# Phi less its first feature is made during the cross attention and kept in DRAM; a row of ones is set by a VectorE eviction

## The chip, the cores and the metric

The kernel runs on one core of one Trainium2 chip, as one program. The metric is the device time of the core in microseconds. Before the change three timed runs gave 577.39, 581.51 and 581.21 us (median 581.21). PE is TensorE, DVE is VectorE, ACT is ScalarE, POOL is GpSimd, and SP is the queue that issues every DMA here.

## The reference, cut to what matters

Three residual steps on x (4 batches x 256 tokens x 256 features), each on the layer norm of x:

```
x = x + xattn(ln(x), ctx)    # one head over 4096 context rows a batch, in f32
x = x + attn(ln(x))          # causal, 16 heads of 16
x = x + ffn(ln(x))           # soft mixture of 64 experts x 32 slots

# ffn:
logits = ln(x) @ phi_w.T + phi_b          # phi_w 2048 x 256, phi_b 2048
D = softmax(logits over the 32 slots);  C = softmax(logits over the 64 experts)
X = D' x -> clip -> norm -> tanh -> expert_w, expert_b -> C mixes the experts' outputs
```

The features of a normed token sum to zero. So every column of phi_w may have its first feature subtracted from all features without changing the logits, and the first feature's row, now zero, is free to carry phi_b, if the first feature of every token is replaced by a one. "Phi less its first feature" is that product: `phi - phi[0]` with row 0 of its first half replaced by phi_b.

## The kernel before, in words

There are three stages, each a block of five engine programs written out in order, and no engine starts a stage before all have ended the one before.

**Cross attention** (`cross_attention`) walks over 4 batches x 8 context chunks of 512 rows. Each chunk comes by two DMAs on SP: turned (512 KB, L325, used for the scores) and plain (512 KB, L321, used for the mix). Both have a ring of four slots. ACT rounds each to f32r (L661, L666), POOL makes the low part (L380, L385), PE multiplies. The low part of turned chunk n+2 and the plain chunk n-6 are made in POOL's iteration n. SP's iteration n loads plain chunk n-6, which waits until the low part four chunks back is done, and turned chunk n. At n = 16, 18 and 20 SP also issues the loads of the self-attention's weights.

**Self attention** (`self_attention`) goes through 16 groups G of 4 heads (4 groups a batch). For each group PE makes the scores, DVE the maxima (L1391), ACT the exponentials with their sums (L1327, L1333), DVE the reciprocals (L1399), POOL multiplies (`normalise(G)`: L1077 then L1080), PE turns the result (L1203, L1204, L1208; here T(G)), ACT and DVE move it to SBUF (L1340, L1404), PE mixes the values. In iteration i the engines do: PE scores of i+2, T(i), mix(i-1); POOL normalise(i+1), at some i the padding of values (L1071), and for i >= 8 `less_first_column(i-8)` (L1090), a subtraction on 128x512 of phi; DVE the maxima of i+2, the evictions of T(i), the maxima of i+3, and in i = 8 and 12 `normed(0)` and `normed(1)` (L1444), the normed tokens of a batch; in i = 6, 10, 14 `add_output`. ACT does the exponentials of i+2 before its eviction of T(i). Phi itself (2 MB, L1053) and its first row broadcast (1 MB, L1054) are loaded on SP when the scores of group 7 are made, `less_first_column` waits for both, and when four of the eight are done phi_b is loaded over row 0 (L1056). At the end POOL writes ones into row 0 of the first half of the turned tokens (L1128).

**Soft mixture** (`soft_moe`) goes through 32 logit units u (token tile x 512 columns): PE (L1740), ACT eviction (L1858), DVE maximum, subtraction, sum and reciprocal (L1945, L1950, L1957, L1962), ACT exponential, POOL division (L1666), PE partial products (L1747). Tokens of the second half are turned by PE after unit 4 (L1732); DVE evicts the first feature half (L1988) as step v = 5, POOL then writes a row of ones into it (L1701), and PE waits for that before it goes on after unit 7.

Of the kernel before, what the change touches and what calls it, by code (L numbers as in the profile page):

```python
# [41 lines left out]
           "phi_in", "x_one_g") + tuple(f"rows_in{k}" for k in range(8))  # L42
# [166 lines left out]
def cross_attention(nc, x_sb, x_stats, x_mv, ident, kept, x_rows, ctx, ctx_turned, w_qk_rows, b_rows, Wv, Wo, bo,  # L209
                    c_attn_w, c_attn_b, c_proj_w, c_proj_b, qk_dram):  # L210

    SCALE = 1.0 / 16.0
    ATT_SCALE = 16 ** -0.5
    RING = 3
    with ExitStack() as st:
# [25 lines left out]
        mv = early[:, DH * D + D + 6 * TT:DH * D + D + 8 * TT].rearrange("p (t e) -> p t e", e=2)  # L241
        ve = sb("ve", [P, TT])
# [32 lines left out]
        wq_a = sem("wq_a")  # L275
# [40 lines left out]
        def _(sp):  # L316
# [10 lines left out]

            def weight(w, a, done):
                sp.dma_start(w_nat[w], a.rearrange("(j p) d -> p j d", p=P)).then_inc(done, 16)
# [29 lines left out]
            for s in range(3):  # L359
                store_parts(sp, kept, qk_dram, parts(s), s)  # L360
                if s == 0:
                    sp.wait_ge(ctxTlo_g, NCH * B)
                if s < 2:
                    stack_rows(sp, kept, qk_dram, q_rows, k_rows, s)

        @block.gpsimd
        def _(pool):
# [32 lines left out]
            for n in range(NCH, B * NCH):  # L400
# [572 lines left out]
def self_attention(nc, x_sb, x_stats, x_mv, x_ve, x_rstd, ident, kept, more, qk_dram, phi_turned, phi_b):  # L973
# [4 lines left out]
    with ExitStack() as st:  # L978
# [57 lines left out]
        SL = phi_b.shape[0]  # L1036
        phi_row = more[:, 4, :]
        phi_in, phi_g, x_one_g = kept.sem["phi_in"], sem("phi_g"), kept.sem["x_one_g"]
# [4 lines left out]
        def _(sp):  # L1043
# [9 lines left out]
            sp.dma_start(kept.front[:], phi_turned).then_inc(phi_in, 16)  # L1053
            sp.dma_start(phi_row, phi_turned[0:1, 0:SL].broadcast_to([P, SL])).then_inc(phi_in, 16)  # L1054
            sp.wait_ge(phi_g, SL // 512)
            sp.dma_start(kept.front[0:1, 0:SL], phi_b.rearrange("(o s) -> o s", o=1)).then_inc(phi_in, 16)  # L1056
            sp.wait_ge(phi_in, 48)

        @block.gpsimd
        def _(pool):  # L1060
# [43 lines left out]
            for i in range(GROUPS):  # L1104
# [20 lines left out]
                if i >= GROUPS // 2:  # L1125
                    less_first_column(i - GROUPS // 2)
# [382 lines left out]
def soft_moe(nc, x_sb, x_stats, x_mv, x_ve, x_rstd, ident, kept, disp, expert_w, expert_b, out):  # L1509
# [18 lines left out]
    with ExitStack() as st:  # L1528
# [10 lines left out]
        power = sb("power3", [P, QT])  # L1539
        sstats = sb("sstats", [P, 2, 6])  # L1540
# [115 lines left out]
        def _(pool):  # L1656
# [71 lines left out]
        def _(pe):  # L1728
# [64 lines left out]
            for u in range(NU):  # L1793
                if u == 3:
                    pe.wait_ge(kept.sem["out_v"], B)
                logit(u)
# [3 lines left out]
                if u == LB + 3:  # L1800
                    pe.wait_ge(x_one_g, 2)
# [128 lines left out]
        def _(dve):  # L1930
# [4 lines left out]

            add_projection(dve, nc, kept, x_sb, B - 1)
# [41 lines left out]
            for v in range(NU + 1):  # L1978
# [57 lines left out]
def perceiver_block(nc, x_rows, ctx, ctx_turned, w_qk_rows, b_rows, Wv, Wo, bo, c_attn_w, c_attn_b, c_proj_w, c_proj_b,  # L2036
                    phi_turned, phi_b, expert_w, expert_b, out):
    SL = phi_b.shape[0]
    with ExitStack() as st:
# [13 lines left out]
        qk_dram = nc.dram_tensor("qk_parts_dram", (2 * DH, 2, NPART, P, HALF), BF16).ap()  # L2053
        with ExitStack() as until_moe:
            kept = carried_tensors(nc, until_moe, bank, front, back, first, phib, wide, turned)
            cross_attention(nc, x_sb, x_stats, x_mv, ident, kept, x_rows, ctx, ctx_turned, w_qk_rows, b_rows, Wv, Wo, bo,
                            c_attn_w, c_attn_b, c_proj_w, c_proj_b, qk_dram)
            more = st.enter_context(nc.sbuf_tensor("more", [P, TT - 2, SL], F32))
            self_attention(nc, x_sb, x_stats, x_mv, x_ve, x_rstd, ident, kept, more, qk_dram, phi_turned, phi_b)
# [28 lines left out]
```

## Time and profile before

| | us |
|---|---|
| timed runs | 577.39, 581.51, 581.21 (median 581.21) |
| profiled execution, its own time | 578.23 |
| its span | 576.4 |
| PE busy | 541.2 (94%) |
| DVE / ACT / POOL busy | 345.5 / 357.7 / 350.6 |
| mean granted TensorE clock | 0.994 of full |

The span is from the first to the last instruction of one execution taken by the hardware profiler; the 1.8 us beside it are start and end. Busy shares are averages over the three stages, which lie at 0 to 262 us, 262 to 362 us and 362 to 576 us. PE is busy nearly throughout the first and the third; in the second its slices go down to 7 or 8 tenths.

### The profile page before, as it was taken

To read this page: it belongs to the slowest core of one execution; us is meant where nothing else is said; L and a number is where in the kernel's file an instruction comes from. 1 tells how busy PE (TensorE), PEld (TensorE's weight loads), DVE (VectorE), ACT (ScalarE), POOL (GpSimd) and SP (SyncE) were. 2 spreads that over 40 slices of the span, in tenths; PEclk is the share of its full clock that TensorE was granted. 3 is DMA by queue.
4 is the path that set the end of the run, shared out by engine and by line. 5 is a ranking of instruction groups with operands and counts; after the bars stand their busy time and mean duration, and the time that the engine had idled before them with its cause. 6 is when DMAs were issued, how large, how long until landed. Compare 5 with 4: busy or idle time off the path is not lost. (4 is left out here: it accounts for less than half of the span.)

```text
span 576.4 us, 9531 instructions
## 1 busy us (share of the span) xinstructions
PE 541.2 (94%) x3384; PEld 429.5 (75%) x3384; DVE 345.5 (60%) x695; ACT 357.7 (62%) x1000; POOL 350.6 (61%) x271
## 2 busy tenths in 40 slices
PE   5998999999999999998997977879999999999998
PEld 4786998999899999887666655445555886777786
DVE  1784444464456445536787896787999999334100
ACT  2437665766576857853887973339999885554300
POOL 2775986667666764644579697244576889906000
PEclk9999999999999999999899998999999999999999
DMA  8454445454434333176069400400000907877100
GB/s 290 155 220 147 147 146 182 149 202 146 162 131 146 146 117 103 48 148 136 2 169 213 168 2 0 148 1 1 0 1 1 195 24 232 280 218 221 38 19 18
DMA packets 37056, 70.22 MB, mean 122 GB/s; under 512 B 3217, under 2 KB 27153, under 8 KB 35985
## 3 DMA queue, kind: packets, MB, share of 16 engines
q1 hardware_dynamic: 37010, 69.62, 39.3%
q8 instruction: 27, 0.44, 0.3%
q14 instruction: 19, 0.16, 0.1%
HBM read 65.42 MB, written 4.19 MB: 121 GB/s over the span
## 5 line engine op out<-in xcount | busy, mean ns | idle before, releaser
L380 POOL TENSOR_TENSOR ctxT_lo<-front,ctxT_hi 128x1024 fp32r<-128x1024 f32 x32 | 76.8, 2405 | 55.3 <-ACT ctxT_hi L661 55.3
L385 POOL TENSOR_TENSOR ctx_lo<-ctx_in,ctx_hi 128x1024 fp32r<-128x1024 f32 x32 | 76.7, 2400 | 17.2 <-ACT ctx_hi L666 17.2
L494 PE MATMUL ps<-ctx_hi,pT_hi 128*128 128x256 f32 x256 | 75.4, 295 | 1.8 <-DVE pT_lo L832 1.8
L496 PE MATMUL ps<-ctx_hi,pT_lo 128*128 128x256 f32 x256 | 72.4, 283 | 0.0
L495 PE MATMUL ps<-ctx_lo,pT_hi 128*128 128x256 f32 x256 | 72.3, 283 | 0.0
L685 ACT CAST pT_hi<-ps 128x512 fp32r<-128x512 f32 x64 | 34.0, 591 | 42.1 <-PE ps L476 42.1
L1740 PE MATMUL ps<-front,turned 128*128 128x512 f32 x128 | 59.7, 593 | 0.3 <-PEq L978 0.3
L1788 PE MATMUL ps<-front,comb 128*128 128x256 f32 x256 | 57.8, 381 | 0.0
L824 DVE TENSOR_SCALAR_CACHE_REDUCE first<-ps,qbk 128x512 f32<-128x512 f32 x32 | 24.0, 750 | 55.5 <-PE ps L464 53.1
L1788 PEld LDWEIGHTS ps<-front,comb 128*128 128x128 f32 x256 | 47.6, 190 | 7.6 <-issue 1.6
L832 DVE TENSOR_TENSOR pT_lo<-ps,pT_hi 128x512 fp32r<-128x512 f32 x64 | 41.1, 686 | 17.4 <-ACT pT_hi L685 17.4
L494 PEld LDWEIGHTS ps<-ctx_hi,pT_hi 128*128 128x128 f32 x256 | 49.0, 191 | 2.8 <-DVE pT_lo L832 2.5
L1869 ACT ACTIVATE comb<-comb,cneg 128x64 f32<-128x64 f32 x128 | 51.0, 417 | 0.0
L1679 POOL TENSOR_TENSOR comb<-comb,cinv 128x512 f32<-128x512 f32 x32 | 40.2, 1283 | 15.5 <-DVE cinv L1975 15.5
L495 PEld LDWEIGHTS ps<-ctx_lo,pT_hi 128*128 128x128 f32 x256 | 49.1, 192 | 0.1
L496 PEld LDWEIGHTS ps<-ctx_hi,pT_lo 128*128 128x128 f32 x256 | 49.0, 191 | 0.0
L464 PE MATMUL ps<-ctxT_hi,qk_hi 128*128 128x512 f32 x128 | 40.7, 400 | 2.6 <-DVE qk_lo L816 2.2
L464 PE MATMUL ps<-ctxT_lo,qk_hi 128*128 128x512 f32 x128 | 39.7, 391 | 0.0
L464 PE MATMUL ps<-ctxT_hi,qk_lo 128*128 128x512 f32 x128 | 39.7, 391 | 0.0
L1740 PEld LDWEIGHTS ps<-front,turned 128*128 128x128 f32 x128 | 24.1, 190 | 19.4 <-issue 17.9
L1666 POOL TENSOR_TENSOR more<-more,dinv 128x512 f32<-128x512 f32 x24 | 25.1, 1048 | 19.6 <-DVE dinv L1962 19.6
L661 ACT CAST ctxT_hi<-front 128x1024 fp32r<-128x1024 f32 x32 | 33.8, 1060 | 5.1 <-PE ps L464 3.8
(235 smaller groups left out, 1345.2 us busy)
## 6 DMA issues: line engine op xcount, KB each, us to landing
front<-in_ctx_turned_dram SPq DMA_DIRECT2D x32, 512.0 KB, 4.3
ctx_in<-in_ctx_dram SPq DMA_DIRECT2D x32, 512.0 KB, 3.3
back<-in_L_ffn_expert_w_dram SPq DMA_DIRECT2D x11, 1024.0 KB, 5.5
turned<-in_L_ffn_expert_w_dram SPq DMA_DIRECT2D x5, 1024.0 KB, 7.7
front<-in_phi_turned_dram SPq DMA_DIRECT2D x1, 2048.0 KB
front<-in_L_ffn_expert_b_dram SPq DMA_DIRECT2D x4, 512.0 KB, 10.3
qk_parts_dram<-first SPq DMA_DIRECT2D x4, 384.0 KB, 5.1
qk_parts_dram<-qk_parts SPq DMA_DIRECT2D x4, 384.0 KB, 2.9
```

Source lines behind the costliest of these rows:

```text
L380: nc.gpsimd.tensor_tensor(ctxT_lo[:, n % RING, :, :], turned_in[:, n % SLOTS, :, :], ctxT_hi[:, n % RING, :, :].bitcast(F32), ALU.subtract ...
L385: nc.gpsimd.tensor_tensor(ctx_lo[:, m % RING, :], ctx_in_sb[:, m % SLOTS, :], ctx_hi[:, m % RING, :].bitcast(F32), ALU.subtract).then_inc( ...
L464: last = nc.tensor.matmul(pS[q][:], a[:, dh, q * P:(q + 1) * P], k[:, n % RING, dh, :], start=step == 0, stop=step == 5)
L494: nc.tensor.matmul(pO[q][:, 0:D], pT_hi[:, c % 2, q, cols], hi, start=c == 0 and j == 0, stop=False)
L495: nc.tensor.matmul(pO[q][:, 0:D], pT_hi[:, c % 2, q, cols], lo, start=False, stop=False)
L496: last = nc.tensor.matmul(pO[q][:, 0:D], pT_lo[:, c % 2, q, cols], hi, start=False, stop=c == NCH - 1 and j == J - 1)
L685: nc.scalar.copy(pT_hi[:, c % 2, q, :], probs_banks(c)[q][:]).then_inc(probsThi_a, 1)
L832: nc.vector.tensor_tensor(pT_lo[:, c % 2, q, :], probs_banks(c)[q][:], pT_hi[:, c % 2, q, :].bitcast(F32), ALU.subtract).then_inc(probsTlo ...
L1679: nc.gpsimd.tensor_tensor(part, part, cinv[:, c, :].unsqueeze(1).broadcast_to([P, EB, NS]), ALU.mult).then_inc(cmul_g, 1)
L1740: last = nc.tensor.matmul(psL[u % 4][:], hT[:, c, t * P:(t + 1) * P], phiT[:, c, cols], start=c == 0, stop=c == DH - 1)
L1788: last = nc.tensor.matmul(psY[t], comb[:, t, s * P:(s + 1) * P], mixed[:, s, :], start=s == 0 and (t >= TT // 2 or t % 2 == 0), stop=s == ...
L1869: nc.scalar.activation(column, column, ACT.Exp, bias=cneg[:, c, p:p + 1], accum_out=csum[:, c, p:p + 1]).then_inc(cslot_a, 1)
```

## The change

In the cross attention SP loads phi in four pieces of 128x1024 (iterations n = 14, 18, 22, 26) together with its first row, broadcast, POOL subtracts in its iterations n = 12, 16, 20, 24 (behind the low parts of that iteration), and SP stores the piece in DRAM three iterations after its load (n = 17, 21, 25, 29), and phi_b into row 0. `load_phi(k)` waits until store k-1 has landed. In the self attention one DMA of 2 MB brings the product in; the eight POOL subtractions, the broadcast load and the load of phi_b are gone. In the mixture the ones of the second half come from the eviction itself: DVE multiplies by a column that is 0 in partition 0 and 1 elsewhere and adds a column that is 1 in partition 0 and 0 elsewhere. The first column is made at the start of the stage.

```
+PIECE_AT, PIECE_EVERY = 2 * NCH - 2, 4
+phi_piece = sb("phi_piece", [P, 2, PIECE])                    # PIECE = 1024
 # cross attention, SP
+def load_phi(k):
+    at_least(sp, phi_out, 16 * k)
+    sp.dma_start(phi_piece[:, 0, :], phi_turned[:, k * PIECE:(k + 1) * PIECE]).then_inc(phi_in, 16)
+    sp.dma_start(phi_piece[:, 1, :], phi_turned[0:1, cols].broadcast_to([P, PIECE])).then_inc(phi_in, 16)
+def store_phi(k):
+    first = 1 if k < 2 else 0
+    sp.wait_ge(phi_g, k + 1)
+    sp.dma_start(phi_dram[first:, k * PIECE:(k + 1) * PIECE], phi_piece[first:, 0, :]).then_inc(phi_out, 16)
+    if k == 3:
+        sp.dma_start(phi_dram[0:1, 0:SL], phi_b.rearrange("(o s) -> o s", o=1)).then_inc(phi_out, 16)
 for n in range(NCH + 2, B * NCH):
     load(n - 6)
     load_turned(n)
+    k, step = divmod(n - PIECE_AT, PIECE_EVERY)
+    if 0 <= k < 4 and step == 0:
+        load_phi(k)
+    if 0 <= k < 4 and step == 3:
+        store_phi(k)
...
+sp.wait_ge(phi_out, 16 * (4 + 1))
 # cross attention, POOL, end of iteration n
+k, step = divmod(n + 2 - PIECE_AT, PIECE_EVERY)
+if 0 <= k < 4 and step == 0:
+    pool.wait_ge(phi_in, 32 * (k + 1))
+    nc.gpsimd.tensor_tensor(phi_piece[:, 0, :], phi_piece[:, 0, :], phi_piece[:, 1, :], ALU.subtract).then_inc(phi_g, 1)
 # self attention, SP
 sp.wait_ge(s_mm, 3 * 2 * NG)
-sp.dma_start(kept.front[:], phi_turned).then_inc(phi_in, 16)
-sp.dma_start(phi_row, phi_turned[0:1, 0:SL].broadcast_to([P, SL])).then_inc(phi_in, 16)
-sp.wait_ge(phi_g, SL // 512)
-sp.dma_start(kept.front[0:1, 0:SL], phi_b.rearrange("(o s) -> o s", o=1)).then_inc(phi_in, 16)
-sp.wait_ge(phi_in, 48)
+sp.dma_start(kept.front[:], phi_dram).then_inc(phi_in, 16)
+sp.wait_ge(phi_in, 16)
 # self attention, POOL
-def less_first_column(k):
-    pool.wait_ge(phi_in, 32)
-    part = kept.front[:, k * 512:(k + 1) * 512]
-    nc.gpsimd.tensor_tensor(part, part, phi_row[:, k % 4 * 512:(k % 4 + 1) * 512], ALU.subtract).then_inc(phi_g, 1)
...
-    if i >= GROUPS // 2:
-        less_first_column(i - GROUPS // 2)
 # mixture, POOL
-if u == LB:
-    pool.wait_ge(pro_v, 1)
-    nc.gpsimd.memset(hT[0:1, 0, HALF:2 * HALF], 1.0).then_inc(x_one_g, 1)
 # mixture, PE
+if u == 0:
+    pe.wait_ge(x_one_g, 1)
...
 if u == LB + 3:
-    pe.wait_ge(x_one_g, 2)
+    pe.wait_ge(pro_v, 2)
 # mixture, DVE, first instruction
+nc.vector.tensor_scalar(rest_rows[:], ident[:, 0:1], -1.0, 1.0, ALU.mult, ALU.add).then_inc(pro_v, 1)
...
 if v == LB + 1:
     dve.wait_ge(pro_mm, 1)
-    nc.vector.tensor_copy(hT[:, 0, HALF:2 * HALF], PS_TURN[0][:]).then_inc(pro_v, 1)
+    dve.wait_ge(pro_v, 1)
+    nc.vector.tensor_scalar(hT[:, 0, HALF:2 * HALF], PS_TURN[0][:], rest_rows[:], ident[:, 0:1],
+                            ALU.mult, ALU.add).then_inc(pro_v, 1)
```

## Rows read from the trace of the kernel before

**Rows 1.** Stretches: us, busy PE, PEld, DVE, ACT, POOL; clock, DMA share, GB/s.

```profile
308.60:325.30 16.70, 14.90 (x144) 10.75 (x145) 12.74 (x31) 12.82 (x59) 10.58 (x15) 1.00 0.87 255
60.00:186.00 126.00, 126.00 (x833) 114.79 (x832) 62.39 (x138) 81.01 (x150) 89.78 (x42) 1.00 0.46 161
...
325.00:348.00 23.00, 19.36 (x188) 13.30 (x188) 20.39 (x35) 16.50 (x73) 22.74 (x26) 1.00 0.01 2
348.00:362.00 14.00, 9.94 (x89) 7.31 (x88) 7.33 (x17) 5.40 (x15) 8.53 (x11) 0.88 0.00 0
```

**Rows 2.** Waits in 290 to 362 us: waiter <- releaser: total us, times, longest us.

```profile
ACT eB L1333 <- DVE nmax L1391: 10.4, 7, 4.1
...
PE ps L1203 <- ACT pT L1340: 3.4, 1, 3.4
```

**Rows 3.** Instructions of L1090 and of L1444: durations in ns min/median/max, first and last start.

```profile
L1090 POOL TENSOR_TENSOR front<-front,more x8: 1260/1270/1278, 325.3 to 357.4; 128x512 f32<-128x512 f32 x8
...
L1444 DVE TENSOR_SCALAR wide<-x_sb,x_mv,x_rstd x4: 400/409/5078, 323.6 to 347.9; 128x256 f32<-128x256 f32 x4
```

**Rows 4.** Timeline of PE, starts of T(10), (11), (13), (14), (15); start, duration, [idle].

```profile
329.44 0.33 PE L1203 MATMUL ps<-ident,eA 128*128 128x128 f32 x1 [0.17 <-POOL eB L1080]
...
334.24 0.33 PE L1203 MATMUL ps<-ident,eA 128*128 128x128 f32 x1 [1.27 <-POOL eB L1080]
...
343.77 0.33 PE L1203 MATMUL ps<-ident,eA 128*128 128x128 f32 x1 [1.05 <-POOL eB L1080]
...
345.23 0.64 PE L1220 MATMUL ps<-pT,v_pad 128*32 128x256 f32 x8
...
346.02 1.99 PE L1232 MATMUL ps<-w_proj,h1T 128*128 128x256 f32 x8
351.43 0.39 PE L1203 MATMUL ps<-ident,eA 128*128 128x128 f32 x1 [3.41 <-ACT pT L1340]
...
355.75 0.27 PE L1203 MATMUL ps<-ident,eA 128*128 128x128 f32 x1
```

**Rows 5.** Timeline of POOL: end of normalise(9), then two phi subtractions.

```profile
319.00 1.90 POOL L1080 TENSOR_TENSOR eB<-eB,rinv 128x1024 f32<-128x1024 f32 x1 [0.87 <-DVE rinv L1399]
325.26 1.28 POOL L1090 TENSOR_TENSOR front<-front,more 128x512 f32<-128x512 f32 x1 [4.37 <-DMA more<-in_phi_turned_dram]
...
343.68 1.27 POOL L1090 TENSOR_TENSOR front<-front,more 128x512 f32<-128x512 f32 x1
```

**Rows 6.** Timeline of DVE, iteration i = 12 and the first maxima of i = 13.

```profile
342.22 0.17 DVE L1399 RECIPROCAL rinv<-esum 128x4 f32<-128x4 f32 x1
...
342.88 5.40 DVE L1444 TENSOR_SCALAR wide<-x_sb,x_mv,x_rstd 128x256 f32<-128x256 f32 x2
348.20 0.68 DVE L1391 TENSOR_REDUCE nmax<-ps 128x2 f32<-128x512 f32 x1
```

**Rows 7.** Cross attention: POOL around iteration n = 12, SP's turned load 15, ACT's use of it.

```profile
83.51 2.39 POOL L385 TENSOR_TENSOR ctx_lo<-ctx_in,ctx_hi 128x1024 fp32r<-128x1024 f32 x1
87.65 2.40 POOL L380 TENSOR_TENSOR ctxT_lo<-front,ctxT_hi 128x1024 fp32r<-128x1024 f32 x1 [1.75 <-ACT ctxT_hi L661]
...
73.31 0.43 SPq L325 DMA_DIRECT2D front<-in_ctx_turned_dram  x1
79.44 0.33 SPq L321 DMA_DIRECT2D ctx_in<-in_ctx_dram  x1
...
86.52 1.06 ACT L661 CAST ctxT_hi<-front 128x1024 fp32r<-128x1024 f32 x1
```

**Rows 8.** Cross attention: a small DVE operation beside POOL (L870), durations in ns min/median/max.

```profile
L870 DVE TENSOR_SCALAR ve<-x_mv x3: 269/271/2066, 114.2 to 228.3; 128x2 f32<-128x2 f32 x3
```

**Rows 9.** Mixture, timelines of DVE and PE: the eviction, PE's next work.

```profile
382.11 0.68 DVE L1988 COPY turned<-ps 128x512 f32<-128x512 f32 x1
...
383.43 1.13 PE L1747 MATMUL ps<-wide,first 128*128 128x256 f32 x4 [3.02 <-POOL turned L1701]
```

**Rows 10.** DVE on PSUM with a column operand: durations in ns min/median/max.

```profile
L824 DVE TENSOR_SCALAR_CACHE_REDUCE first<-ps,qbk x32: 740/750/752, 19.3 to 212.5; 128x512 f32<-128x512 f32 x32
```

More of the change, by code:

```diff
@@ L41 @@
            "h2T_mm", "h2T_a", "qk2_mm", "high_a", "rest_v", "middle_a", "low_g", "parts_out0", "parts_out1", "frows_v", "focus_v",
-           "phi_in", "x_one_g") + tuple(f"rows_in{k}" for k in range(8))
+           "x_one_g") + tuple(f"rows_in{k}" for k in range(8))
 def at_least(eng, sem, value):
@@ L209, in cross_attention @@
 def cross_attention(nc, x_sb, x_stats, x_mv, ident, kept, x_rows, ctx, ctx_turned, w_qk_rows, b_rows, Wv, Wo, bo,
-                    c_attn_w, c_attn_b, c_proj_w, c_proj_b, qk_dram):
+                    c_attn_w, c_attn_b, c_proj_w, c_proj_b, phi_turned, phi_b, qk_dram, phi_dram):
     SCALE = 1.0 / 16.0
     ATT_SCALE = 16 ** -0.5
+    SL = phi_b.shape[0]
+    PIECE = SL // 2
+    PIECE_AT, PIECE_EVERY = 2 * NCH - 2, 4
     RING = 3
@@ L274, in cross_attention @@
          rest_v, middle_a, low_g) = (kept.sem[n] for n in SIGNALS[2:22])
-        wq_a = sem("wq_a")
+        phi_in, phi_g, phi_out, wq_a = sem("phi_in"), sem("phi_g"), sem("phi_out"), sem("wq_a")
         wide_v, weights_mm, weights_a, small_v = sem("wide_v"), sem("weights_mm"), sem("weights_a"), sem("small_v")
@@ L326, in load_turned @@
                     ctxT_in[n % SLOTS], 16)
+            def load_phi(k):
+                at_least(sp, phi_out, 16 * k)
+                cols = slice(k % 2 * PIECE, (k % 2 + 1) * PIECE)
+                sp.dma_start(phi_piece[:, 0, :], phi_turned[:, k * PIECE:(k + 1) * PIECE]).then_inc(phi_in, 16)
[6 more added lines that the diff above has]
+                    sp.dma_start(phi_dram[0:1, 0:SL], phi_b.rearrange("(o s) -> o s", o=1)).then_inc(phi_out, 16)
             def weight(w, a, done):
@@ L970, in _, with self_attention @@
             invert_sums(LAST)
-def self_attention(nc, x_sb, x_stats, x_mv, x_ve, x_rstd, ident, kept, more, qk_dram, phi_turned, phi_b):
+def self_attention(nc, x_sb, x_stats, x_mv, x_ve, x_rstd, ident, kept, more, qk_dram, phi_dram):
     MASKED = -3.0e38
@@ L1035, in self_attention @@
         xhT_mm, xhT_a = sem("xhT_mm"), sem("xhT_a")
-        SL = phi_b.shape[0]
-        phi_row = more[:, 4, :]
-        phi_in, phi_g, x_one_g = kept.sem["phi_in"], sem("phi_g"), kept.sem["x_one_g"]
+        phi_in, x_one_g = sem("phi2_in"), kept.sem["x_one_g"]
         block = st.enter_context(nc.Block())
@@ L1539, in soft_moe @@
         power = sb("power3", [P, QT])
+        rest_rows = sb("rest_rows", [P, 1])
         sstats = sb("sstats", [P, 2, 6])
@@ L2053, in perceiver_block @@
         qk_dram = nc.dram_tensor("qk_parts_dram", (2 * DH, 2, NPART, P, HALF), BF16).ap()
+        phi_dram = nc.dram_tensor("phi_less_dram", (P, DH * SL), F32).ap()
         with ExitStack() as until_moe:
@@ L2056, in perceiver_block @@
             cross_attention(nc, x_sb, x_stats, x_mv, ident, kept, x_rows, ctx, ctx_turned, w_qk_rows, b_rows, Wv, Wo, bo,
-                            c_attn_w, c_attn_b, c_proj_w, c_proj_b, qk_dram)
+                            c_attn_w, c_attn_b, c_proj_w, c_proj_b, phi_turned, phi_b, qk_dram, phi_dram)
             more = st.enter_context(nc.sbuf_tensor("more", [P, TT - 2, SL], F32))
-            self_attention(nc, x_sb, x_stats, x_mv, x_ve, x_rstd, ident, kept, more, qk_dram, phi_turned, phi_b)
+            self_attention(nc, x_sb, x_stats, x_mv, x_ve, x_rstd, ident, kept, more, qk_dram, phi_dram)
         disp = [first[:, t * SL:(t + 1) * SL] for t in range(2)] + [more[:, t, :] for t in range(TT - 2)]
```

## The prediction

> **What bounds the kernel now.** I read the table by stretch first. From 60 to 186 us, where the four pieces of phi will be made, PE is busy for all of its 126 us, POOL for 89.8 of them, and the DMAs move 161 GB/s at 46% of their time [rows 1]. There POOL has room and PE has none to give. From 325 to 348 us it is the other way round: POOL is busy 22.74 of 23 us, PE 19.36 [rows 1]. That is the stretch of the eight phi subtractions, so the change takes work from POOL where POOL is full and gives it back where it is not.
>
> The list of waits then says what ends PE's pauses [rows 2]: PE waited once 3.4 us for ACT's eviction, and ACT in its turn had waited up to 4.1 us for a DVE maximum. Three shorter pauses of PE, 0.17, 1.27 and 1.05 us, end with POOL's normalise [rows 4], and POOL had stood 4.37 us for the phi load [rows 5]. The timelines explain the long one. DVE's maximum is late because `normed(1)` before it on DVE takes 5.40 us for two operations [rows 6] of which the fastest takes 0.400 us; one took 5.078 us [rows 3]. During it POOL runs back to back: the phi subtraction at 343.68 follows normalise(13) and precedes normalise(14) without a gap [rows 5]. `normed(0)` met POOL standing in its wait for phi, and was quick. After this stall the granted clock of 348 to 362 us is 0.88 [rows 1], so part of that stretch ran at the lower level (1.2 GHz). In the mixture the chain of work that ended last goes from DVE's eviction through POOL's row of ones to PE [rows 9], and is PE almost alone behind that, to the end.
>
> **Part 1, POOL's phi work leaves the self attention.** Removed: 8 x 1.270 = 10.2 us of POOL [rows 3] and the wait of 4.37 us [rows 5]. I follow T(10), (11), (13), (14), (15), which start at 329.44, 334.24, 343.77, 351.43 and 355.75 [rows 4].
> - T(10) to T(13). POOL's own delays before them are 0.17, 1.27 and 1.05 us [rows 4]; the long wait for phi was mostly absorbed, because the output projection of batch 1 keeps PE busy there. Without POOL, T(13) is next bound by the chain of exponentials on ACT and maxima on DVE. It falls by at least the last pause, 1.05, at most by their sum, 2.5; I take 1.5, nearer to the last, since groups not held by POOL came hardly closer.
> - The start of `normed(1)`. DVE reaches it behind two iterations paced by ACT, so only about 0.4 us earlier, at 342.5. POOL now has no backlog: the second half of normalise(14) starts when the reciprocal before it is done, 342.22 + 0.17 less 0.4, that is 342.0 [rows 6], takes 1.9 (as at 319.00) [rows 5] and ends at 343.9. If `normed(1)` is blocked until then, its two operations of 0.4 end at 344.7, overlapping slightly; I say 344.5, against 348.20 before [rows 6]: 3.7 us sooner.
> - T(14). From DVE's maximum at 348.20 to T(14) at 351.43 are 3.23 us of maximum, exponentials and eviction [rows 4, 6], which stay: 344.5 + 3.2 = 347.7, a gain of 3.7 at T(14). The 1.5 at T(13) is contained in it.
> - T(15). T(14) to T(15) took 4.32 us with the clock partly down. PE's pause before T(14) began at 351.43 - 3.41 = 348.0 and will begin at 346.5, so it shrinks to 1.2 us; I take it that the clock stays up. The same work at full clock is 2.8 us: the twelve turns 1.46 (343.77 to 345.23), the mix 0.79 (to 346.02) [rows 4], four turns of normed tokens a third of twelve, 0.5. Gain 1.5, total **5.2 us** at T(15). What follows up to the mixture keeps its length.
> - Against it: in i = 8 POOL no longer stands still, so `normed(0)` now falls beside normalise(10) and may be blocked, at most for one 1.90 [rows 5], about 1.4 us. Its cover is the output projection on PE (8 products after T(9)) which paced T(10); if that cover is gone, 0.4 to 1.4 us of the gain are lost. I take none.
>
> Here a rule speaks against the change. The Trainium skill (SBUF — State Buffer, "Who interferes with whom") says that VectorE in a two-port mode and GpSimd lock a shared pair of ports, for the whole instruction, and that the later one blocks fully. The trace agrees that blocking exists (0.400 against 5.078 us) [rows 3], but the block there lasts over several POOL instructions, not one. By the rule alone, one instruction at most, `normed(1)` would have cost at most 1.9 more, and nothing of this gain could be explained.
>
> **Part 2, the phi work in the cross attention.** POOL gets 4 subtractions of 128x1024, like L385 at 2.39 us [rows 7]: 9.6 us. The first begins at 85.9 and ends at 88.3; the next low part began at 87.65 after an idle 1.75 [rows 7], so it slips 0.65 us, and PE needs that chunk more than one chunk (6.5 us) later. On the path: 0. If the cover were gone, 0.65 x 4 = 2.6 us. DVE has small SBUF operations that can be held up by POOL: L870 took 0.27 twice and 2.07 once [rows 8], and two of the four subtractions follow right behind it. Bounds 0 to 2 x 2.4; DVE idles between a chunk's score evictions, so I take 0.
>
> **Part 3, the queue.** SP issues twelve more DMAs of 512 KB and one small one. The tightest neighbour is turned chunk 15: asked for just after 79.44, first used by ACT at 86.52 [rows 7]. In front of it will stand the context chunk asked for by 73.31 (1.05 MB), phi's 1.05 MB, and its own plain chunk. At the 255 GB/s that the DMAs reached while phi was loaded before [rows 1], four times 0.52 MB take 8.2 us, to 81.5; with the next pair 85.6, in time by 0.9 us, and POOL's first subtraction at 85.9 has its data. Stores wait for a subtraction that is done by then; the wait of `load_phi` on the landed store holds up only that SP iteration, whose loads have been issued. Cost 0 to 5.6 (at 1.4 each); I take 0.2, since the margin is thin. In the self attention the load is 2 MB rather than 3, and is not awaited before the mixture: 0. The end of the cross attention gets one wait long fulfilled: 0.
>
> **Part 4, the row of ones.** DVE ended at 382.11 + 0.68 = 382.79, PE began at 383.43 [rows 9]: 0.64 us of POOL's work and two hand-overs, of which one hand-over stays, about 0.1 (an estimate; 0 to 0.3). The eviction goes from 0.68 to about 0.75, the price of L824, which reads PSUM with a column [rows 9, 10]. Net gain 0.45, between 0.3 and 0.57. The column `rest_rows` costs about the 0.17 of the reciprocal on 128x4 [rows 6] at the head of DVE, which then waits for ACT's eviction of the first logits: 0, at most 0.17. The wait of PE at unit 0 is for a thing done before the stage ends: 0.
>
> **Sum:** 5.2 - 0.2 + 0.45 = 5.4 us. Against the profiled execution's 578.23 that is 572.8; against the median of 581.21 it is 575.8. The four executions shown lie at 577.4 to 578.2 and at 581.2 to 581.5, half each; I forecast 575.5, near the median.
>
> **Rivals.**
> - A, the block stays: DVE's `normed(1)` again falls among back-to-back POOL work (normalise(14), then the paddings) or `normed(0)` takes over the stall. The length of POOL's run decides; for it speaks that of the POOL work beside the 5.40 us only 1.27 was phi's, against it that the reciprocals now gate normalise. Then T(14) gains 0.4, the clock still drops, and all is 0.9: 580.3 (577.3 on the profile's level). The lock rule of the page named above would bring it so if both norms were hit. Chance 0.18.
> - B, more: every pause of PE for POOL and ACT goes (2.5 + 3.4) [rows 2, 4], the clock gives 1.5, the ones 0.45: 7.9, 573.3 (570.3). For it speaks that DVE and ACT gain slack too, 20.39 and 16.50 busy of 23 us [rows 1]; against, that DVE at 20.39 is itself nearly full. Chance 0.17.
> - C, slower: phi's loads hold back the context stream. If they get only what 255 leaves beside 161 GB/s, about 100 [rows 1], a piece takes 10 us and not 4.1; chunk 15 lands at 91.5, ACT may give 1.75 us beyond 86.52, the idle time that POOL shows behind it [rows 7], so 3.2 us are lost four times, 12.8 - 5.4 = 7.4: 588.6. It decides from the point where a piece takes over 6.8 us, and beats the gain over 8.1. Against it: busy at 46% for 161 GB/s, the DMAs have more to give. Chance 0.08.
>
> **How the numbers follow.** The forecast has 0.57, on its own range 572.5 to 578.5. About 1%, 5.8 us, is what a measurement of this kernel can tell from no change. The forecast lies just under that border: 0.30 above, 0.27 below. Faster: 0.30 + 0.17 (B) = 0.47. Same: 0.27 + 0.18 (A) + 0.01 of C = 0.46. Slower: 0.07. The range takes in A at its upper end, 580.3, and B on the profile's level, 570.3, and leaves C out: 570 to 580.5.
>
> **What would show it.** Right: no POOL wait at 321 to 325; `normed(1)` under 2.5 us for its two operations; ACT's wait for a maximum in i = 13 under 1 us; T(15) 5 us sooner after T(9); clock near 1.0 before the mixture; PE's pause near 380 us shorter by 0.45; the cross attention of the same length, ACT's L661 without DMA waits. Wrong: `normed(0)` or `normed(1)` at 4 us or more (A), or the cross attention longer by over 1 us (C, or DVE held up by POOL).

## The result, and the profile after

The changed kernel takes 605.34 us (median of four runs, 603.46 to 606.08) against 580.19 for the kernel before on the same chip (four runs, 577.39 to 581.51). The ratio is 1.0435, 95% interval 1.0387 to 1.0484: slower by 25 us. The forecast of 575.5 with a range of 570 to 580.5 was wrong. The profiled execution after took 603.46, with a span of 601.7 and a mean granted clock of 0.974; the one before had a span of 576.4 and 0.994.

**Where the time went** comes from three landmarks in each timeline: the clearing of `causal` on POOL, which is its first instruction in the self attention; the add of `b_proj` on POOL, which stands in iteration 5 of the self attention, ahead of everything that the change touches there; and the first logits on PE, where the mixture begins. The last line is PE's product behind the row of ones. The kernel after; start, duration, engine, line:

```profile
291.02 0.20 POOL L1083 MEMSET causal<- 128x128 bf16 x1 [2.79 <-POOLq L218]
...
338.25 1.26 POOL L1131 TENSOR_TENSOR x_sb<-x_sb,b_proj 128x512 f32<-128x512 f32 x1
...
387.79 8.82 PE L1753 MATMUL ps<-front,turned 128*128 128x512 f32 x20 [0.32 <-PEq L1005]
...
408.50 1.13 PE L1760 MATMUL ps<-wide,first 128*128 128x256 f32 x4 [2.56 <-DVE turned L2005]
```

The same three landmarks in the kernel before:

```profile
260.31 0.20 POOL L1061 MEMSET causal<- 128x128 bf16 x1 [2.80 <-POOLq L215]
...
307.13 1.27 POOL L1114 TENSOR_TENSOR x_sb<-x_sb,b_proj 128x512 f32<-128x512 f32 x1
...
362.26 8.82 PE L1740 MATMUL ps<-front,turned 128*128 128x512 f32 x20 [0.32 <-PEq L978]
```

The cross attention became 30.7 us longer (260.31 to 291.02), and up to the second landmark it is 31.1 (307.13 to 338.25). From there to the mixture it took 55.13 and takes 49.54: 5.6 us less. From the first logits to the product after the row of ones it took 21.17 [rows 9] and takes 20.71: 0.46 less. So the two gains that the prediction counts came, and a stage to which it gave 0.2 us ate them five times over.

Stretches of the cross attention say when: duration, busy us of PE, PEld, DVE, ACT and POOL, granted clock, DMA share and GB/s. After, then before:

```profile
96.00:121.00 25.00, 21.55 (x128) 18.74 (x126) 11.19 (x31) 8.33 (x17) 8.30 (x4) 0.99 0.28 105
121.00:141.00 20.00, 11.86 (x59) 11.03 (x60) 4.08 (x8) 9.70 (x17) 11.77 (x6) 0.67 0.64 213
141.00:166.00 25.00, 18.09 (x119) 16.17 (x118) 11.98 (x19) 8.26 (x16) 10.15 (x5) 0.91 0.28 103
166.00:186.00 20.00, 14.09 (x86) 13.18 (x87) 4.87 (x9) 10.99 (x18) 15.02 (x7) 0.77 0.59 197
```
```profile
96.00:121.00 25.00, 25.00 (x160) 22.51 (x159) 12.59 (x33) 15.10 (x30) 13.90 (x7) 1.00 0.63 206
121.00:141.00 20.00, 20.00 (x136) 18.28 (x135) 11.18 (x20) 13.66 (x27) 15.48 (x8) 1.00 0.44 158
```

PE, full before, pauses. From 96 to 121 us the DMAs move half of the bytes that they moved before (105 against 206 GB/s) and catch up in the next stretch, and the same pattern comes again from 141 us. Behind each pause the granted clock is down (0.67, 0.77), so part of those stretches ran at its lower level (1.2 GHz). The list of waits names the thing that came late (waiter <- releaser: total us, times, longest us):

```profile
POOL ctxT_lo L403 <- ACT ctxT_hi L688: 76.8, 24, 17.5
...
ACT ctxT_hi L688 <- DMA front<-in_ctx_turned_dram: 38.3, 7, 15.0
...
PE ps L503 <- ACT wide L703: 24.4, 3, 12.8
...
SPq L335 <- DMA phi_less_dram<-phi_piece: 26.9, 3, 13.5
```

ACT waits 38.3 us for context chunks, seven times; in the kernel before it waited once, 1.3 us. PE in turn waits 24.4 us for ACT in one line. The timeline of SP around the first store, of the kernel after (`phi_less_dram` is the DRAM tensor that holds the product; L341 is the store of phi's piece, L325 and L329 the two context loads, L335 the next load of phi):

```profile
96.36 0.33 SPq L341 DMA_DIRECT2D phi_less_dram<-phi_piece  x1
99.54 7.45 SPq L325 DMA_DIRECT2D ctx_in<-in_ctx_dram  x1
107.03 0.43 SPq L329 DMA_DIRECT2D front<-in_ctx_turned_dram  x1
121.02 0.33 SPq L335 DMA_DIRECT2D phi_piece<-in_phi_turned_dram  x1
```

L335 waits for the landing of the store, so the store of 508 KB landed 24.7 us after its issue; the second one, issued at 141.82, held L335 until 166.55, 24.7 us again. Beside the first the issue of one context load took 7.45 us on SP instead of 0.33. The view of the DMAs for 90 to 130 us (40 slices of 1 us; busy tenths of the 16 DMA engines, and GB/s) shows what moved meanwhile; the two rows below it give the means of two of its stretches (columns as in the table of stretches above), and the last is ACT's first use of the chunk whose load was issued at 107.03:

```profile
DMA  8210114995000000058960000000000179950027
GB/s 313 54 35 15 34 33 115 356 373 213 20 25 29 25 29 25 29 135 311 418 238 29 25 29 25 25 37 25 29 25 29 37 209 287 406 165 1 0 53 154
```
```profile
100.00:107.00 7.00, 7.00 (x48) 6.38 (x47) 3.37 (x8) 5.62 (x13) 4.51 (x2) 1.00 0.07 26
111.00:121.00 10.00, 6.55 (x41) 5.61 (x39) 4.51 (x13) 0.00 (x0) 0.00 (x0) 0.98 0.07 27
```
```profile
123.63 1.05 ACT L688 CAST ctxT_hi<-front 128x1024 fp32r<-128x1024 f32 x1 [14.31 <-DMA front<-in_ctx_turned_dram]
```

From 100 to 107 us and from 111 to 121 the traffic is 26 and 27 GB/s with a busy share of 0.07, about what one DMA engine of 16 makes when it alone is busy (1/16 is 0.06). In between, from 107 to 111, up to 418 GB/s are reached. I read that as the parts of the context loads that belong to the other engines; the chunk issued at 107.03 is then complete only when the one engine has come to its part of it. The landing times fit: the loads of L329 took 3.1/5.3/16.5 us to land (min/median/max; 3.3/4.3/9.6 before), and ACT starts on that chunk at 123.63, after 14.31 us of idling.

The store is `phi_piece[first:]` with `first = 1` for the pieces 0 and 1: 127 rows. The third piece, of 128 rows, was stored at 182.89, and the load that waits for it was issued at 189.24, 6.4 us later.

The Trainium skill (DMA: Bandwidth & Descriptors, "Why a DMA increments its semaphore by 16 and not by 1") says that a DMA is spread over the largest number of engines up to 16 that divides the outermost dimension of both sides, and gives 127 as a case that gets one. The trace agrees: a busy share of 0.07 of the 16 engines and 26 to 27 GB/s while the store of 127 rows is under way. The rule was there to be read, and the prediction did not weigh it.

In the self attention the forecast's landmarks, of the kernel after: starts of T(10), T(11), T(13), T(14) and T(15), then DVE's norms (L1459, ns min/median/max).

```profile
360.21 0.27 PE L1218 MATMUL ps<-ident,eA 128*128 128x128 f32 x1
...
363.97 0.30 PE L1218 MATMUL ps<-ident,eA 128*128 128x128 f32 x1
...
373.31 0.30 PE L1218 MATMUL ps<-ident,eA 128*128 128x128 f32 x1
...
378.54 0.30 PE L1218 MATMUL ps<-ident,eA 128*128 128x128 f32 x1 [0.33 <-ACT pT L1355]
...
381.25 0.27 PE L1218 MATMUL ps<-ident,eA 128*128 128x128 f32 x1
```
```profile
L1459 DVE TENSOR_SCALAR wide<-x_sb,x_mv,x_rstd x4: 401/1016/1631, 354.7 to 375.0; 128x256 f32<-128x256 f32 x4
```

Counted from the add of `b_proj`, and set against [rows 4], they come 0.35, 1.39, 1.58, 4.01 and 5.62 us sooner. From T(14) to T(15) PE takes 2.71 us where it took 4.32, and the granted clock from 378.5 to 381.5 us is 1.00.

### The profile page after: what moved, and what is told of

Its sections match the earlier page's. It is cut to its first block and busy times, and to the rows that moved or that the text cites. A ratio compares the mean times of both kernels' runs of the same rounds, so it can differ in the third digit from the quotient of the medians.

```text
span 601.7 us, 9540 instructions
## 1 busy us (share of the span) xinstructions
PE 545.6 (91%) x3384; PEld 433.3 (72%) x3384; DVE 343.4 (57%) x696; ACT 358.6 (60%) x1000; POOL 350.0 (58%) x266
## 5 line engine op out<-in xcount | busy, mean ns | idle before, releaser
L521 PE MATMUL ps<-ctx_hi,pT_hi 128*128 128x256 f32 x256 | 76.9, 301 | 1.8 <-DVE pT_lo L859 1.8
L688 ACT CAST ctxT_hi<-front 128x1024 fp32r<-128x1024 f32 x32 | 33.7, 1056 | 42.1 <-DMA front<-in_ctx_turned_dram 38.3
L503 PE MATMUL ps<-ident,wide 128*128 128x128 f32 x256 | 35.4, 287 | 24.4 <-ACT wide L703 24.4
L503 PEld LDWEIGHTS ps<-ident,wide 128*128 128x128 f32 x256 | 31.4, 148 | 30.1 <-ACT wide L703 25.7
L521 PEld LDWEIGHTS ps<-ctx_hi,pT_hi 128*128 128x128 f32 x256 | 50.5, 197 | 2.8 <-DVE pT_lo L859 2.5
L522 PEld LDWEIGHTS ps<-ctx_lo,pT_hi 128*128 128x128 f32 x256 | 50.5, 197 | 0.1
```

The costliest lines, as they stand in the source:

```text
L503: last = nc.tensor.transpose(to[q][:, j * P:(j + 1) * P], probs[:, c % 2, q, j * P:(j + 1) * P], ident[:])
L521: nc.tensor.matmul(pO[q][:, 0:D], pT_hi[:, c % 2, q, cols], hi, start=c == 0 and j == 0, stop=False)
L522: nc.tensor.matmul(pO[q][:, 0:D], pT_hi[:, c % 2, q, cols], lo, start=False, stop=False)
```

## The experiments

All times are against the kernel before on the same chip. Fourteen kernels in four groups.

### Is it the number of rows?

**full128**: all four stores take 128 rows; row 0, written with the wrong value, is overwritten by the copy of `phi_b` that the changed kernel has anyway.

```
 # store_phi(k)
-                first = 1 if k < 2 else 0
+                first = 0
```

> The changed kernel, but the stores of pieces 0 and 1 take all 128 partitions and not 127 (row 0 is overwritten by phi_b later anyway, so the same bytes end up in DRAM). Theory S (the 127-row stores are slow in themselves, 24.7 us to landing, and hold SP): the two waits of the phi load fall to about 0 to 3 us, the cross attention is within 1 us of the kernel before, the span about 571, the time 573 to 576, 0.990 of the kernel before. Rival C (the traffic of phi's loads and stores holds back the context stream): bytes and number of DMAs are the same, so it stays at 603 to 606. Rival Q (any store into DRAM that a load waits for takes this long): also 603 to 606.

Measured: 573.22 us (six runs, 572.00 to 576.35) against 579.67, ratio 0.9903, interval 0.9869 to 0.9937. One row more in two stores takes 32 us off the changed kernel. SP's timeline, the waits of ACT, and the DMAs of 90 to 130 us, in this kernel:

```profile
95.81 0.43 SPq L341 DMA_DIRECT2D phi_less_dram<-phi_piece  x1
...
102.08 0.33 SPq L335 DMA_DIRECT2D phi_piece<-in_phi_turned_dram  x1
```
```profile
ACT ctxT_hi L688 <- DMA front<-in_ctx_turned_dram: 2.1, 3, 1.4
```
```profile
GB/s 106 19 32 34 34 65 242 250 184 307 430 410 422 418 418 397 161 9 17 47 94 111 110 343 410 270 373 393 356 336 235 83 2 0 0 127 332 209 274 410
```

The store lands within 6.3 us, in traffic of 184 to 430 GB/s. The whole interval of the ratio lies under 1, so this kernel beats the kernel before, by 1%. Its median is the lowest here, though rows126, self_only, pool8 and wait_only below lie within 0.8 us of it and can't be told from it.

**rows127_from0** (127 rows again, now 0 to 126; row 127 of the first half is copied at the end without the subtraction) and **rows126** (rows 2 to 127; row 1 copied without it). In short, not the code as it stands:

```
rows127_from0:  phi_piece[0:127, 0, :]  -> phi_dram[0:127, ...]
rows126:        phi_piece[2:, 0, :]     -> phi_dram[2:, ...]
```

> The changed kernel with the stores of pieces 0 and 1 still 127 rows long, but rows 0 to 126 and not 1 to 127; row 127 comes by one 8 KB copy at the end, from phi as it was, so one feature's row is left without the subtraction. Theory S, if it is the number of rows that counts: as slow as the changed kernel, 603 to 606, landing after 24 to 25 us. If it is the start at partition 1 (theory P): near 575.

> The changed kernel with the stores of pieces 0 and 1 of 126 rows, 2 to 127; row 1 comes by one 8 KB copy at the end, without the subtraction. If it is the odd or indivisible number of rows that counts (theory S with the rule that a transfer is spread over the largest number up to 16 that divides its rows, 14 here), the store lands in 3 to 6 us and the time is near 575. If only the whole of 128 rows is quick, or the start off partition 0 costs (theory P), it stays at 600 or more.

Measured: 606.74 us (ratio 1.0472, interval 1.0417 to 1.0526; store at 100.22, next load at 124.91) and 573.67 us (0.9901, 0.9869 to 0.9933; 96.15 and 102.31). So it is not that row 0 is left out, nor that a store starts off row 0. Stores of 127 rows are slow at either start, and 126 rows have nothing of it.

**split**: the same 127 rows as two stores, of 15 rows and of 112.

```
 # store_phi(k), for k < 2
+                    sp.dma_start(phi_dram[1:16, cols], phi_piece[1:16, 0, :]).then_inc(phi_out, 16)
+                    sp.dma_start(phi_dram[16:, cols], phi_piece[16:, 0, :]).then_inc(phi_out, 16)
```

> The changed kernel with the same 127 rows stored, but in two DMAs of 15 and of 112 rows. By theory S both are quick (spread over 15 and 16 DMA engines): near 575, landing in 3 to 6 us. If leaving out row 0 as such is what costs, it stays above 600.

Measured: 575.80 us (eight runs, 572.14 to 580.01), ratio 0.9917, interval 0.9877 to 0.9957; stores at 96.81 and 97.33, the next load at 102.69. The same bytes in two DMAs cost nothing that shows.

### The slow store, or the wait for it?

In the changed kernel two things can make the context late: the one engine that carries the store also has a share of every context load behind it (my reading above), and SP stands still until the store has landed.

**two_buf**: the stores keep their 127 rows, but phi's pieces have two buffers, so that the load of piece k waits for the store of piece k - 2.

```
 # load_phi(k)
-                at_least(sp, phi_out, 16 * k)
+                at_least(sp, phi_out[k % 2], 16 * (k // 2))
...
```

> The changed kernel, 127-row stores kept, but two buffers for the piece, so that the load of piece k waits for store k-2, which has landed long before. If the whole loss is the wait that SP stands in (theory W), the 25 us are gone: near 575. If the slow store also holds up the context loads that are issued behind it, because each of them has a share on the DMA engine that is busy with the store (theory R), a good part stays: 585 to 600, with ACT waiting for context DMAs though SP issues them in time. I expect R to be there in part, near 590: in the trace one context load took 7.45 us to issue while the store was under way, before SP came to the wait.

Measured: 602.41 us, ratio 1.0397, interval 1.0348 to 1.0446. The expectation, about 590, failed: with two buffers the context loads are nearly as late as with one. SP's timeline in this kernel:

```profile
99.03 7.96 SPq L325 DMA_DIRECT2D ctx_in<-in_ctx_dram  x1
...
107.50 3.20 SPq L335 DMA_DIRECT2D phi_piece<-in_phi_turned_dram  x1
110.74 1.32 SPq L336 DMA_DIRECT2D phi_piece<-in_phi_turned_dram  x1
112.10 11.27 SPq L196 DMA_DIRECT2D b_qk<-in_L_attn_c_attn_b_dram  x16
```

SP now stands in the issue of what follows, 24 us for four lines, and ACT's wait for the context is 37.0 us, longest 16.2.

**store127_one**, **store127_quarter**, **store127_two**: the kernel before, with spare stores that nothing waits for but the end of the stage; nothing else is changed.

```
+                if n == 2 * NCH + 1:
+                    sp.wait_ge(h1T_a, B)
+                    sp.dma_start(spare_dram[1:, 0:1024], h1T[1:, 0, 0:1024]).then_inc(spare_out, 16)
```

The quarter takes 256 columns instead of 1024; the third kernel issues the full store at two places, four iterations apart. The wait for `h1T_a`, the data of the store, is fulfilled long before.

> The kernel before with one more DMA on SP in iteration n = 17 of the cross attention: 127 rows of 4 KB of the turned tokens into a spare DRAM tensor; nothing waits for it but the end of the stage. It is the disputed store by itself. By what the kernel with two buffers showed (the store holds up the context loads issued behind it, waits of SP or not), one such store costs half of 28 us: 12 to 15 us, 592 to 595. By the theory that only the wait for the store costs, nothing: 580.

> The same as store127_one with 127 rows of 1 KB, a quarter of the bytes. If the store runs at a fixed rate of one DMA engine (520 KB in 24.7 us), this takes 6 us, which the margins of the context stream hide: 579 to 582. If the count of rows and not of bytes sets its length, the cost is as in store127_one.

Measured: one store 589.59 us (ratio 1.0184, interval 1.0138 to 1.0231), one of a quarter of the bytes 580.39 (1.0008, 0.9953 to 1.0063). One store with no other change costs 10 us, somewhat less than the 12 to 15 expected, and the theory that only the wait costs is out. A quarter of it costs nothing that the runs can tell (the interval allows 3.6 us). ACT in store127_one:

```profile
ACT ctxT_hi L666 <- DMA front<-in_ctx_turned_dram: 16.6, 3, 14.7
```

In store127_quarter the same wait is 2.5 us in all.

> Kernel before, with two stores of 127 rows by 4 KB each, issued by SyncE ahead of the context loads of groups 17 and 21, and waited for by nobody; no phi loads are added, no subtraction, no wait. If the loss of the changed kernel lies in the one DMA engine that such a store occupies, this costs twice what one such store cost (2 x 10 us, less what the two overlap): 598 to 602 us against 580. If half of the loss comes from SyncE's wait for the landed store and the second load of phi's pieces, it stays near 590, since the second store would fall in work that the first has already delayed.

Measured: 605.24 us, ratio 1.0398, interval 1.0228 to 1.0569 (three runs before, spread from 577.76 to 584.32, so the traces carry more here). Its landmark, the add of `b_proj`:

```profile
332.81 1.27 POOL L1120 TENSOR_TENSOR x_sb<-x_sb,b_proj 128x512 f32<-128x512 f32 x1
```

That is 25.7 us later than before. In store127_one it is 319.38, 12.3 later; the second store costs 13.4. So the second store costs as much as the first, and the theory by which the time stays near 590 is out. That 605.24 lies above the 598 to 602 expected says little, since the kernel before was slower on this chip too (584.06).

**hold_only**: full128, with SP held at the load of the pieces 1 and 2 until POOL has split a later context group, roughly as long as it stood there in the changed kernel (22.8 us in two waits, 12.3 at most, against 26.9 in three, 13.5 at most). The stores are quick.

```
+                if k in (1, 2):
+                    sp.wait_ge(ctxTlo_g, PIECE_AT + PIECE_EVERY * k + 1)
```

> The version whose stores have 128 rows, with SyncE held before each load of the next piece of phi until the split of context group 19 (23) is done, which is about as long as it stood there in the changed kernel; the stores stay quick. If the wait on SyncE does harm by itself, context loads come late and the time rises to 580 or more. If the harm is in the slow store's DMA engine alone, the time stays at 573 to 577 us.

Measured: 589.49 us (ratio 1.0128, interval 0.9975 to 1.0281, with the same three runs before). The interval does not decide it, the traces do: the landmark lies at 322.94 against 307.10 in full128, 15.8 later, and ACT has two long pauses.

```profile
127.99 1.04 ACT L690 CAST ctxT_hi<-front 128x1024 fp32r<-128x1024 f32 x1 [9.00 <-DMA front<-in_ctx_turned_dram]
...
160.16 1.04 ACT L690 CAST ctxT_hi<-front 128x1024 fp32r<-128x1024 f32 x1 [6.58 <-DMA front<-in_ctx_turned_dram]
```

Their sum is 15.6. So two such waits on SP, by themselves and without any slow store, cost 15 to 16 us (15 when both traces are counted from the load ahead of the first store, as in the table below). The first hold moves the next context load on SP from 110.37 in full128 to 120.77 here:

```profile
120.77 0.42 SPq L325 DMA_DIRECT2D ctx_in<-in_ctx_dram  x1
```

In the kernel before that load was issued at 106.46, so full128 is 3.9 us late with it and loses nothing; 10.4 more cost ACT 9.0. My belief that the wait is harmless at any length fell too.

The landmark in one trace has to be read with care: the traces differ already before the first store. The last turned context load ahead of it is issued at 95.55 us in the kernel before, but at 100.39 in store127_quarter, whose landmark lies at 311.29, and at 99.75 in rows127_from0. Counted from that load, the way to the landmark is longer than in the kernel before by:

| | us |
|---|---|
| full128 | 0.2 |
| store127_quarter | -0.7 |
| store127_one | 11.4 |
| store127_two | 24.9 |
| two_buf | 27.8 |
| the changed kernel | 30.8 |
| rows127_from0 | 30.4 |
| hold_only | 14.7 |

The account is then: two slow stores that nobody waits for, 24.9. With the phi traffic and two buffers, 27.8. With the wait on SP, 30.8. Wait and slow engine delay the same context loads, so their prices (14.7 and 24.9 alone) don't add. The two steps of 3 us are differences of single traces and are not explained by a run of their own. Nor do the runs part what a slow store costs by its share in the loads behind it from what it costs by holding up their issue on SP: in store127_one both happen.

### What gave the gain in the self attention

**self_only**: the kernel before with one load of phi instead of two and neither subtraction nor copy of `phi_b`; it leaves the subtraction and the bias out.

> The kernel before with phi loaded as it is, in one DMA, and nothing else: the eight POOL subtractions, the broadcast load and phi_b are left out (so the subtraction and the bias of the logits are left out). This is part 1 alone. The forecast was 5.2 us; in the trace of the changed kernel the self attention from a POOL operation in group 5 to the start of the mixture is 5.6 us shorter. Theory: 5.2 to 5.8 us less than before, 0.990. Rival A (the block of DVE stays): 0 to 1 us less.

Measured: 573.62 us, ratio 0.9897, interval 0.9853 to 0.9941, mixture from 357.03 (before 362.26), 49.52 us behind the add of `b_proj` where the changed kernel has 49.54. Taking the work out of the self attention alone gives the whole 5.6 us, and its time can't be told from that of full128.

Two kernels take away one half of it. **pool8** is full128 with eight spare subtractions on POOL at the old places, which wait for nothing:

```
+                if i >= GROUPS // 2:
+                    k = i - GROUPS // 2
+                    nc.gpsimd.tensor_tensor(more[:, 4 + k // 4, k % 4 * 512:(k % 4 + 1) * 512], w_qkv[:, 0, 0:512], w_qkv[:, 1, 0:512],
+                                            ALU.subtract).then_inc(spare_g, 1)
```

**wait_only** is the kernel before, in which POOL still waits for both loads of phi, but then does none of the eight subtractions; they and `phi_b` are left out.

```
-                    less_first_column(i - GROUPS // 2)
+                if i == GROUPS // 2:
+                    pool.wait_ge(phi_in, 32)
```

> The changed kernel with 128-row stores, and in the self attention eight POOL subtractions of 128x512 on spare data at the places where the phi subtractions stood, with no wait for any load. It tells POOL's eight operations from POOL's wait for the load. If POOL's length without a gap blocks DVE's norm (my part 1), the 5.08 us operation of DVE is back and 4 to 6 us of the gain are gone: 578 to 580. If the wait for phi was the cause, the time stays at 573 to 576.

> The kernel before with the eight subtractions and the load of phi_b left out (so neither the subtraction nor the bias is made), but POOL still waits in group 8 for phi and for its broadcast row. It is the wait without the operations. If the wait alone brings the 5 us operation of DVE back: 578 to 580. If it takes both, wait and eight operations: 573 to 576. I think both are needed, since without the operations POOL catches up in two groups.

Measured: pool8 573.64 us (0.9891, 0.9833 to 0.9949), wait_only 573.93 us (0.9899, 0.9862 to 0.9937). The expectation of pool8 was missed: 10 us of POOL work put back cost nothing that can be told. DVE's norm in wait_only, against 400/409/5078 in [rows 3]:

```profile
L1442 DVE TENSOR_SCALAR wide<-x_sb,x_mv,x_rstd x4: 402/404/1627, 323.8 to 344.2; 128x256 f32<-128x256 f32 x4
```

With POOL's wait alone or, as in pool8, with the eight operations alone the norm stays under 1.9 us (pool8: 1822 ns at most). With both it is blocked for 5.07 to 5.08 us, in each of the five kernels here whose self attention is that of before (before, ones_only and the three with spare stores).

The timelines show what the two together do. In the kernel before POOL is one group behind when `normed(1)` comes. DVE's long operation, and POOL at its end:

```profile
342.88 5.08 DVE L1444 TENSOR_SCALAR wide<-x_sb,x_mv,x_rstd 128x256 f32<-128x256 f32 x1
```
```profile
345.91 1.89 POOL L1080 TENSOR_TENSOR eB<-eB,rinv 128x1024 f32<-128x1024 f32 x1
347.75 0.99 POOL L1071 COPY v_pad<-wide 128x64 f32<-128x64 f32 x4
```

In pool8:

```profile
342.13 1.82 DVE L1464 TENSOR_SCALAR wide<-x_sb,x_mv,x_rstd 128x256 f32<-128x256 f32 x1
```
```profile
341.91 1.89 POOL L1103 TENSOR_TENSOR eB<-eB,rinv 128x1024 f32<-128x1024 f32 x1
343.75 0.98 POOL L1094 COPY v_pad<-wide 128x64 f32<-128x64 f32 x4
```

In both DVE comes while POOL is in the second half of a normalise, and its operation ends 0.2 us after the padding copies (L1071, L1094) have begun. In the kernel before that half is normalise(13)'s, and a phi subtraction and all of normalise(14) follow it without a gap, until 347.8. In pool8 it is normalise(14)'s, and the copies follow at once. So by the timelines the wait of 4.4 us puts POOL behind, the eight operations keep it there, and what counts is which of POOL's work then lies beside the norm. No run shifts POOL alone to test this.

**late_phi**: the kernel before, with the first subtraction one iteration later, behind normalise, so that POOL does not stand for phi; plus the new row of ones. No round trip of phi through DRAM.

```
 # POOL, self attention
+                if i > GROUPS // 2:
+                    less_first_column(i - GROUPS // 2 - 1)
+                if i == GROUPS - 1:
+                    less_first_column(GROUPS // 2 - 1)
-                if i >= GROUPS // 2:
-                    less_first_column(i - GROUPS // 2)
...
```

> The kernel before, phi subtracted in the self attention as there, but from group 9 on instead of 8 (the eighth doubled up in group 15), so that POOL never stands in its wait for the load; and the row of ones set by VectorE. Nothing in the cross attention, no DRAM round trip. If POOL's wait of 4.4 us, and not its eight operations, caused the 5 us block of VectorE, the gain is as large as that of the 128-row kernel: 573 to 575. If the operations count, it is 577 or more.

Measured: 575.27 us (six runs, 575.06 to 575.67), ratio 0.9921, interval 0.9891 to 0.9952. That is 4.3 us less than before, where full128 has 6.4 less, and the way from the add of `b_proj` to the mixture is 51.51 us: 3.6 of the 5.6 us are gained by a reordering of four lines. The time is just over the 573 to 575 of the one theory and under the 577 of the other. Its norm still takes up to 2441 ns, though POOL did not stand for phi, and that operation, beside normalise(14) as in pool8, ends 0.8 us after the padding copies have begun; that is not explained by what the other kernels show.

### The row of ones

**ones_only**: the kernel before with the eviction that writes the row of ones, and the column that it needs.

> The kernel before with the row of ones of the second half set by VectorE's eviction, and nothing else (part 4 alone). Expected: PE's pause before unit 7's products shorter by 0.4 to 0.5 us, the time less by 0.2 to 0.5 us, which the runs can't tell from none.

Measured: 579.45 us (ten runs), ratio 0.9977, interval 0.9944 to 1.0009: no difference that can be told. Its trace has PE's product at 383.10, before 383.43 [rows 9], with the first logits 0.15 later than there: 0.48 gained at that place. The eviction, in the changed kernel:

```profile
L2005 DVE TENSOR_SCALAR turned<-ps,rest_rows,ident x1: 821/821/821, 407.6 to 407.6; 128x512 f32<-128x512 f32 x1
```

## Why the prediction was wrong, point by point

- **Part 3, the queue: the step that failed.** It counted "twelve more DMAs of 512 KB and one small one" and said: "Stores wait for a subtraction that is done by then; the wait of `load_phi` on the landed store holds up only that SP iteration, whose loads have been issued." The first half prices every DMA by its bytes. Two of them have 127 rows and not 128, as `first = 1 if k < 2 else 0` in the diff says, and took 24.7 us where those of 128 took about 6. The term was 0.2 us, its bound 5.6; the cross attention measured 30.7 longer. full128, rows126 and rows127_from0 show that the number of rows decides, with the bytes all but the same.
- **The same sentence's second half** is wrong as well. The loads of that iteration have been issued, but those of the next have not, and SP issues all of them. hold_only shows 15 to 16 us for two such waits. With stores of 128 rows the wait is 2.9 us in all, and then its cost is 0 as forecast: full128's self attention begins at 260.29 against 260.31. I had not said from which landing time on the wait begins to hurt.
- **Rival C** had the right place, the context stream held back by phi, and the right sign, but its mechanism was shared bandwidth, 255 less 161 GB/s, and it gave 588.6. Bandwidth was not short: full128 moves all but the same bytes, at up to 430 GB/s, and loses nothing. What was short was the share of the engines that the store used, 0.07.
- **Part 1, the self attention: right in size, half right in its cause.** Forecast 1.5 at T(13), 3.7 at T(14), 5.2 at T(15); measured 1.58, 4.01, 5.62. PE's pause before T(14), forecast 1.2, is 0.33, and T(14) to T(15), forecast 2.8, takes 2.71 at full clock. The step "POOL now has no backlog" is right, its cause half so: I put the backlog down to POOL's phi work, and pool8 shows that this work alone does no harm. The wait of 4.37 us [rows 5], which I called mostly absorbed, is the other half. Since the change took out both, the forecast came out in spite of it, and that is in part luck. What lies beside `normed(1)` now is what rival A named, normalise(14) and then the paddings, but it blocks the norm for 1.63 us and not for 5. Normed(0) is slower than before, as I had feared, at 1.95 us for its two operations, and the cover that I named (the output projection on PE) held.
- **The lock rule** of the Trainium skill (SBUF — State Buffer, "Who interferes with whom"), blocked for one instruction of the other engine, fits the kernel after: its longest norm is 1.63 us, inside one POOL operation of 1.90. It does not fit the 5.08 us of before, which lasts over a run of POOL operations without a gap, nor the 2.44 us of late_phi. Why a block can last over several operations is not shown by any run.
- **Part 2: 0 held.** In full128, where the four subtractions run at the places forecast, the cross attention is not longer. There the first began at 85.85, forecast 85.9, and the next low part at 88.23, forecast 88.3.
- **Part 4: right.** 0.46 at the product, forecast 0.45, made up a little otherwise: the eviction takes 0.82 us, not 0.75, and the hand-over 0.05 (from 407.63 + 0.82 to 408.50), not 0.1. That these two misses cancel to within 0.01 is luck. At the end of the kernel only 0.23 us of it is left (mixture 214.14 to 213.91), and ones_only cannot tell it from nothing.
- **The sum.** 5.6 + 0.23 less nothing would be 572.4 on the profile's level; full128's profiled execution took 572.27, where the prediction had 572.8. The other terms came near their sizes, and it is the 127 rows that set the result.

## What to carry to other kernels

Read the shape of every DMA that a change adds, not its bytes: a slice like `[1:]` of 128 rows cost 10 to 13 us a time here, and storing the unwanted row too, with a later write over it, cost nothing. When a queue that feeds the critical stage is given a wait, work out from which landing time on its next load is late, and say it. A stall that needs two things at once can be lessened by taking away the cheaper of the two: here a reordering of four lines (and the new row of ones, which alone can't be told from nothing) gives 575.3, where the whole change, with stores of 128 rows, gives 573.2.

## What the runs showed of the hardware

- A store of 127 rows x 4 KB landed after 24.7 us, with stretches in which all DMAs together moved 26 to 27 GB/s at a busy share of 0.07; 126 or 128 rows landed within 6.3 us. With it, loads of 128 rows behind it landed up to 16.5 us after their issue (9.6 at most in the kernel before).
- The issue itself grows: the first context load behind the first store took 7.45 to 8.42 us on SP (changed kernel, two_buf, rows127_from0, store127_one, store127_two) instead of 0.33, and sixteen small loads took 11.27 in two_buf and 12.28 in store127_one, but 5.77 in the kernel before and 5.73 in hold_only. So SP is held even with no wait in the program. Why the first load behind the store is the one that is held long was not tried.
- A quarter of the store (127 x 1 KB) in the same place costs nothing that can be told. That fits a harm that lies in how long the one engine is held, against the slack of the stream.
- DVE's small norm was blocked for 5.07 to 5.08 us only where POOL had first stood 4.1 to 4.5 us for a DMA and then had extra operations to do, so that a run of them without a gap lay beside it; where copies followed the first operation at once it took 1.6 to 1.8 us, and in late_phi 2.4.
